# POOL issues a gather only when the third one in front of it has landed (graph kernel: two LSTM layers and a relational convolution)

## The chip, the cores and the metric

The kernel runs on one core of a Trainium2 chip. The metric is device time in microseconds, the median of the runs of one build: 597.44 us for the kernel before (three runs, 597.39 to 602.68). The names of the engines are those of the profile: PE (TensorE; PEld is its weight load), DVE (VectorE), ACT (ScalarE), POOL (GpSimd), SP (SyncE, which here only starts DMAs). Each has its own queue of instructions, and they meet through semaphores.

## The reference

Two graph layers, each with its own residual and layer norm. The first aggregates the neighbours with an LSTM, twice (weights `conv1`, `conv2`), the second multiplies each edge's source row with one of three relation matrices and sums over the target node.

```python
def _lstm_last(seq, wih, whh, bih, bhh):       # seq: 33 steps x 512 nodes x 128
    def step(carry, x_t):
        h, c = carry
        g = x_t @ wih.T + h @ whh.T + b
        i, f, gg, o = jnp.split(g, 4, axis=-1)
        c = sigmoid(f) * c + sigmoid(i) * jnp.tanh(gg)
        h = sigmoid(o) * jnp.tanh(c)
def _sage_conv(x, src, ...):
    msgs = x[src].reshape(n, d, c)             # 16896 edges = 512 nodes x 33
    aggr = _lstm_last(jnp.swapaxes(msgs, 0, 1), wih, whh, bih, bhh)
    return aggr @ wl.T + bl + x @ wr.T
# layer 1: _sage_conv, relu, _sage_conv; x = layernorm(x + that)
# layer 2: einsum('ni,rio->rno', x, weight); msg = hr[rel, src] * norm
#          h = segment_sum(msg, dst); out = layernorm(x + relu(h))
```

## The kernel before

**LSTM.** The input product of a step needs only the row of a node, so for each of the two LSTM layers `l` the table `gate_table[l]` (512 rows of 512 float32: all nodes times `wih`, plus the biases) is computed once, copied to `table_sb` in SBUF and stored to DRAM by SP. Step `t` then needs, for its 512 nodes, the table rows of their `t`-th neighbours. POOL fetches them with indirect DMAs ("gathers", line 442), four for each step (`K` = 4), 128 rows of 2 KB each, 256 KB in all, into `rows`. `rows` has `DEEP` = 5 turns of four slots, 20 slots (`SLOTS`), and each slot has its semaphore `rows_in[slot]`, which a gather raises by 16 when it has landed. Five of the 33 steps (0, 1, 3, 8 and 17, `BY_ONEHOT`) take their rows on PE with a one-hot matrix instead, so 28 steps of each layer are gathered: 56 turns, 224 gathers.

A turn's first gather waits, from the sixth turn on, for `gates1[1]` of the step that used the same slots five turns ago (line 440): PE raises it with the last recurrent product of a step (line 1066). The first gather of a layer waits for `table_stored`, and in layer 2 for both. The other three of a turn wait for nothing. So a layer begins with a run of 20 gathers, the whole depth of `rows`, and goes on with four for each finished step.

On PE a gathered step is 16 transposes of the gathered rows into the PSUM tile `gates` (line 1059), which wait for `rows_in`, for `if_ready` and `o_ready` (ACT has read what stood there), and then 24 products with `h_hi` and `h_lo` for each half of the step; the 512 nodes are two halves `h` of 256. With the fourth group of them it raises `gates0[h]` and `gates1[h]`. ACT makes of these the gates (`act_if`, `act_g`, `act_o`, lines 509 to 525) and tanh of the cell, DVE the cell and the new `h`, and PE waits for `h_hi_ready` and `h_lo_ready`. The two halves take turns: while ACT and DVE work on one, PE works on the other.

**Relational part.** 132 tiles of 128 edges, in 12 blocks. For 54 of the tiles PE picks the source rows with one-hots (line 1219, into PSUM, taken by ACT into `picked`, line 630) and multiplies them with the three matrices (line 1235). For the other 78 POOL gathers message rows from `msg_table` (line 453, 128 rows of 512 bytes, 64 KB) into `edge_rows`, two blocks deep, with a semaphore `edge_rows_in[c % 2][n]` for each place. From block 3 on a gather waits for `rows_taken` (ACT has read the place two blocks ago). PE sums all messages over the target nodes (line 1242).

POOL has nothing else to do than these 302 gathers, after a few small instructions at the start.

## Time and profile before

| | us |
|---|---|
| median of 3 runs (597.39 to 602.68) | 597.44 |
| the profiled execution's own time | 601.25 |
| its span, from first to last instruction | 599.2 |
| PE busy | 491.3 |
| DVE busy | 380.2 |
| ACT busy | 349.6 |
| POOL busy | 299.1 |
| software DMA queue (the gathers), share of 16 engines | 38.0% |

The profiled execution has 2.05 us outside its span (601.25 less 599.2) and is 3.81 us above the median. Its busy times say how long an engine had an instruction under way; a busy PE is not PE at its peak. Where an engine idled, the profile names what ended the idle time: another engine's instruction, a DMA, "issue" (nothing that the profile shows) or "remote" (an update that it can put down to no instruction near it).

### The profile page before, as it was taken

To read this page: it belongs to the slowest core of one execution; us is meant where nothing else is said; L and a number is where in the kernel's file an instruction comes from. 1 tells how busy PE (TensorE), PEld (TensorE's weight loads), DVE (VectorE), ACT (ScalarE), POOL (GpSimd) and SP (SyncE) were. 2 spreads that over 40 slices of the span, in tenths; PEclk is the share of its full clock that TensorE was granted. 3 is DMA by queue.
4 is the path that set the end of the run, shared out by engine and by line. 5 is a ranking of instruction groups with operands and counts; after the bars stand their busy time and mean duration, and the time that the engine had idled before them with its cause. 6 is when DMAs were issued, how large, how long until landed. Compare 5 with 4: busy or idle time off the path is not lost.

```text
span 599.2 us, 9532 instructions
## 1 busy us (share of the span) xinstructions
PE 491.3 (82%) x3479; PEld 349.7 (58%) x3479; DVE 380.2 (63%) x1040; ACT 349.6 (58%) x896; POOL 299.1 (50%) x312
## 2 busy tenths in 40 slices
PE   8638989788878799729898888878999649788696
PEld 3516767677767685518676667666775315444353
DVE  5306778668666685417677676766787329567384
ACT  4417767557666686417676576656776326447372
POOL 1662555564666500754646645666007746566620
PEclk9957999899999999958999999999999869899989
DMA  4862464574667601664646655666111211111100
GB/s 130 256 200 71 112 185 134 170 196 122 193 181 203 171 8 71 175 175 111 175 126 176 180 152 139 171 180 171 44 37 52 52 33 49 36 49 35 44 14 19
DMA packets 27833, 71.84 MB, mean 120 GB/s; under 512 B 6383, under 2 KB 10405, under 8 KB 27788
## 3 DMA queue, kind: packets, MB, share of 16 engines
q0 software_dynamic: 20416, 63.85, 38.0%
q1 hardware_dynamic: 6284, 6.48, 3.7%
q10 hardware_dynamic: 1088, 0.92, 0.5%
q8 instruction: 28, 0.46, 0.3%
q14 instruction: 17, 0.14, 0.1%
HBM read 68.06 MB, written 3.16 MB: 119 GB/s over the span
## 4 chain that ended last, share of the span: by engine, by line
PE 48%; ACT 17%; another core or an unknown queue 14%; DVE 13%; issue 7%; DVEq 0%; ACTq 0%
PE gates L1066 22%; PE gates L1059 6%; PE work L1242 5%; PE gates L1001 3%; ACT h_hi L505 3%; DVE h_full L756 3%; ACT act_g L521 3%; ACT act_if L509 2%; DVE h_lo L761 2%; DVE prod_ig L779 2%; DVE prod_fc L777 2%; ACT act_o L525 2%; PE gates L1219 2%; PE gates L1235 2%
## 5 line engine op out<-in xcount | busy, mean ns | idle before, releaser
L442 POOL DMA_INDIRECT rows<-gate_table,src_steps x224 | 216.9, 968 | 201.2 <-PE gates L1066 90.8
L1059 PE MATMUL gates<-ident,rows 128*128 128x128 f32 x896 | 122.9, 280 | 54.6 <-ACT act_o L525 29.3
L1059 PEld LDWEIGHTS gates<-ident,rows 128*128 128x128 f32 x896 | 100.2, 143 | 71.7 <-ACT act_o L525 37.2
L1066 PE MATMUL gates<-h_hi,whh_hi 128*128 128x256 f16 x512 | 127.9, 276 | 0.9
L1066 PE MATMUL gates<-h_hi,whh_lo 128*128 128x256 f16 x512 | 127.1, 275 | 0.0
L453 POOL DMA_INDIRECT edge_rows<-msg_table,msg_index x78 | 80.7, 1034 | 74.9 <-DMA msg_table<-table_sb 30.9
L1066 PE MATMUL gates<-h_lo,whh_hi 128*128 128x256 f16 x512 | 99.3, 276 | 0.9 <-DVE h_lo L761 0.9
L777 DVE TENSOR_TENSOR prod_fc<-act_if,cell 128x256 f32<-128x256 f32 x128 | 54.2, 424 | 68.0 <-issue 26.6
L509 ACT ACTIVATE act_if<-gates 128x512 f32<-128x512 f32 x112 | 66.0, 590 | 47.4 <-remote 35.6
L505 ACT ACTIVATE h_hi<-h_full 128x256 f16<-128x256 f32 x128 | 53.4, 417 | 47.2 <-DVE h_full L756 44.0
L779 DVE TENSOR_TENSOR prod_ig<-act_if,act_g 128x256 f32<-128x256 f32 x128 | 53.9, 421 | 37.9 <-issue 22.8
L761 DVE TENSOR_TENSOR h_lo<-h_full,h_hi 128x256 f16<-128x256 f32 x128 | 54.4, 425 | 31.8 <-ACT h_hi L505 18.1
L521 ACT ACTIVATE act_g<-gates 128x256 f32<-128x256 f32 x112 | 42.6, 380 | 33.1 <-PE gates L1066 24.0
L1066 PEld LDWEIGHTS gates<-h_hi,whh_hi 128*128 128x128 f16 x512 | 50.4, 98 | 19.0 <-ACT h_hi L505 10.0
L756 DVE SCALAR_TENSOR_TENSOR h_full<-act_o,tanh_c 128x256 f32<-128x256 f32 x132 | 55.3, 419 | 2.9 <-ACT tanh_c L501 2.4
L501 ACT ACTIVATE tanh_c<-cell 128x256 f32<-128x256 f32 x132 | 54.7, 414 | 1.7 <-DVE cell L785 1.2
L785 DVE TENSOR_TENSOR cell<-prod_ig,prod_fc 128x256 f32<-128x256 f32 x128 | 54.0, 422 | 2.2
L1066 PEld LDWEIGHTS gates<-h_hi,whh_lo 128*128 128x128 f16 x512 | 50.7, 99 | 5.7
L1066 PEld LDWEIGHTS gates<-h_lo,whh_hi 128*128 128x128 f16 x512 | 45.2, 98 | 14.0 <-DVE h_lo L761 1.2
L956 DVE TENSOR_TENSOR msg_lo<-msg_full,msg_hi 128x768 f16<-128x768 f32 (+2 forms) x23 | 21.3, 926 | 34.6 <-ACT msg_hi L657 33.8
L525 ACT ACTIVATE act_o<-gates 128x256 f32<-128x256 f32 x112 | 42.7, 381 | 0.0
L1242 PE MATMUL work<-rows,msg_lo 128*128 128x512 f16 x132 | 34.7, 390 | 8.2 <-issue 8.1
(158 smaller groups left out, 615.7 us busy)
## 6 DMA issues: line engine op xcount, KB each, us to landing
rows<-gate_table,src_steps POOLq DMA_INDIRECT x224
gate_table<-rows SPq DMA_DIRECT2D x8, 256.0 KB, 2.1
edge_rows<-msg_table,msg_index POOLq DMA_INDIRECT x78
code<-code_table SPq DMA_DIRECT2D x5, 160.0 KB
msg_table<-table_sb SPq DMA_DIRECT2D x4, 192.0 KB, 2.5
code<-code_table SPq DMA_DIRECT2D x5, 128.0 KB
whhT<-turned_whh SPq DMA_DIRECT2D x2, 256.0 KB, 2.6
wihT<-turned_wih ACTq DMA_DIRECT2D x1, 256.0 KB, 3.0
```

The lines of the kernel that those rows point to most:

```text
L442: pool.indirect_dma_start(rows[:, j * K + k, :], None, gate_table[l], bass.IndirectOffsetOnAxis(src_steps[:, t, k:k + 1], axis=0)).then_in ...
L453: pool.indirect_dma_start(edge_rows[:, c % 2, n, :], None, msg_rows, bass.IndirectOffsetOnAxis(msg_index[:, pool_first(c) + n:pool_first(c ...
L505: act.activation(h_hi[:, h, :], h_full[:, h, :], ACT.Copy).then_inc(h_hi_ready[h], 1)
L509: act.activation(act_if[:, h, :], gates[:, h, 0, :], ACT.Sigmoid, scale=1 / G_SCALE).then_inc(if_ready[h], 1)
L521: act.activation(act_g[:, h, :], gates[:, h, 1, 0:HN], ACT.Tanh, scale=1 / G_SCALE, bias=bias).then_inc(g_ready[h], 1)
L756: dve.scalar_tensor_tensor(h_full[:, h, :], act_o[:, h, :], H_SCALE, tanh_c[:, h, :], op0=ALU.mult, op1=ALU.mult).then_inc(h_full_ready[h], 1)
L761: dve.tensor_tensor(h_lo[:, h, :], h_full[:, h, :], h_hi[:, h, :], ALU.subtract).then_inc(h_lo_ready[h], 1)
L777: dve.tensor_tensor(prod_fc[:, h, :], act_if[:, h, HN:], cell[:, h, :], ALU.mult)
L779: dve.tensor_tensor(prod_ig[:, h, :], act_if[:, h, 0:HN], act_g[:, h, :], ALU.mult).then_inc(ig_ready[h], 1)
L1059: pe.matmul(gates[:, h, b, q * HN + k * P:q * HN + (k + 1) * P], rows[:, j * K + 2 * h + k, gate * P:(gate + 1) * P], ident[:, :], is_tran ...
L1066: mm = pe.matmul(gates[:, h, b, q * HN:(q + 1) * HN], w[:, gate * P:(gate + 1) * P], state[:, h, :], start=False, stop=last and q == 1, sk ...
L1242: mm = pe.matmul(work[:, 1, :], part[:, k % AHEAD, m, :], dst_onehot[k % AHEAD * GR + m], start=False, stop=False, skip_group_check=True)
```

## The change

A constant `IN_FLIGHT = 3` is added, and POOL waits before each gather, except the first three of each of the two loops, until the gather three places in front of it has landed. In the LSTM loop that order runs on over the turns and over both layers. The waits for slots that are to become free stay. No engine other than POOL gets, loses or moves an instruction.

```diff
+    IN_FLIGHT = 3
@@ gpsimd, LSTM gathers
                 for k in range(K):
+                    if turn * K + k >= IN_FLIGHT:
+                        landed, part = divmod(turn * K + k - IN_FLIGHT, K)
+                        pool.wait_ge(rows_in[landed % DEEP * K + part], 16 * (landed // DEEP + 1))
                     pool.indirect_dma_start(
                         rows[:, j * K + k, :], None, gate_table[l],
@@ gpsimd, gathers of the relational part
+            gathered = [(c, n) for c in range(BLOCKS) for n in range(SIZES[c] - PE_TILES[c])]
             for c in range(BLOCKS):
                 for n in range(SIZES[c] - PE_TILES[c]):
+                    if pool_first(c) + n >= IN_FLIGHT:
+                        landed, slot = gathered[pool_first(c) + n - IN_FLIGHT]
+                        pool.wait_ge(edge_rows_in[landed % 2][slot], 16 * slot_fills(landed, slot))
                     if c >= 3:
                         pool.wait_ge(rows_taken, pool_first(c - 2) + min(n + 1, SIZES[c - 2] - PE_TILES[c - 2]))
```

POOL's queue at the start of LSTM layer 1, before: the run of 20 gathers, and then one turn of four whose first waits for the step.

```order
L442 DMA rows<-gate_table,src_steps 128x512 [waits table_stored,src_loaded]
L442 DMA rows<-gate_table,src_steps 128x512 x19
L442 DMA rows<-gate_table,src_steps 128x512 [waits gates1_1]
L442 DMA rows<-gate_table,src_steps 128x512 x3
L442 DMA rows<-gate_table,src_steps 128x512 [waits gates1_1]
```

The same queue after the change, its first rows and those around the first gather that also waits for `gates1_1` (`rows_in0` to `rows_in19` are the landing semaphores of the 20 slots).

```order
L446 DMA rows<-gate_table,src_steps 128x512 [waits table_stored,src_loaded]
L446 DMA rows<-gate_table,src_steps 128x512 x2
L446 DMA rows<-gate_table,src_steps 128x512 [waits rows_in0]
L446 DMA rows<-gate_table,src_steps 128x512 [waits rows_in1]
```

```order
L446 DMA rows<-gate_table,src_steps 128x512 [waits rows_in16]
L446 DMA rows<-gate_table,src_steps 128x512 [waits rows_in17,gates1_1]
L446 DMA rows<-gate_table,src_steps 128x512 [waits rows_in18]
L446 DMA rows<-gate_table,src_steps 128x512 [waits rows_in19]
L446 DMA rows<-gate_table,src_steps 128x512 [waits rows_in0]
L446 DMA rows<-gate_table,src_steps 128x512 [waits rows_in1,gates1_1]
```

No gather moved. Of the run of 20 the first three are as before and the other 17 wait for a landing; each later gather waits for one too, and those that waited for a step now wait for both. In the relational part POOL's queue was this before (one row stands for 63 gathers):

```order
L453 DMA edge_rows<-msg_table,msg_index 128x128 [waits msg_stored,edge_ready]
L453 DMA edge_rows<-msg_table,msg_index 128x128 x14
L453 DMA edge_rows<-msg_table,msg_index 128x128 [waits rows_taken] x63
```

and is this after, at the place where the wait for `rows_taken` begins:

```order
L461 DMA edge_rows<-msg_table,msg_index 128x128 [waits edge_rows_in0_3]
L461 DMA edge_rows<-msg_table,msg_index 128x128 [waits edge_rows_in0_4]
L461 DMA edge_rows<-msg_table,msg_index 128x128 [waits rows_taken,edge_rows_in0_5]
L461 DMA edge_rows<-msg_table,msg_index 128x128 [waits rows_taken,edge_rows_in0_6]
L461 DMA edge_rows<-msg_table,msg_index 128x128 [waits rows_taken,edge_rows_in0_7]
```

The order of the gathers is the same there too; each of the last 75 of 78 has one wait more.

## Rows read from the trace of the kernel before

**Rows 1.** The page: its head, and busy us of each engine
```profile
span 599.2 us, 9532 instructions
PE 491.3 (82%) x3479; PEld 349.7 (58%) x3479; DVE 380.2 (63%) x1040; ACT 349.6 (58%) x896; POOL 299.1 (50%) x312
```

**Rows 2.** Waits of the whole span: engine line <- releaser: us in total, times, longest
```profile
POOL rows L442 <- PE gates L1066: 90.8, 41, 10.4
...
ACT act_if L509 <- remote: 35.6, 15, 7.2
...
ACT picked L630 <- remote: 29.0, 6, 11.1
...
POOL edge_rows L453 <- issue: 19.0, 61, 0.6
```

**Rows 3.** Stretches: one step with gathers, one without: busy us (instructions), PEclk, DMA, GB/s
```profile
171.39:177.36 5.97, 4.86 (x40) 3.90 (x40) 4.00 (x11) 3.75 (x11) 3.81 (x4) 1.00 0.62 177
212.99:217.53 4.54, 4.54 (x42) 3.95 (x41) 3.80 (x11) 3.74 (x11) 0.00 (x0) 1.00 0.08 22
```

**Rows 4.** Timeline (start, us) of the step with gathers, then of that without
```profile
175.27 0.38 PE L1066 MATMUL gates<-h_lo,whh_hi 128*128 128x256 f16 x2
...
177.13 0.38 ACT L521 ACTIVATE act_g<-gates 128x256 f32<-128x256 f32 x1 [0.87 <-PE gates L1066]
177.36 0.94 POOL L442 DMA_INDIRECT rows<-gate_table,src_steps  x1 [1.24 <-PE gates L1066]
...
215.69 0.38 PE L1066 MATMUL gates<-h_lo,whh_hi 128*128 128x256 f16 x2
...
216.11 0.38 ACT L521 ACTIVATE act_g<-gates 128x256 f32<-128x256 f32 x1
```

**Rows 5.** Timeline of POOL, first run of LSTM layer 1 and the turns behind it
```profile
17.24 1.12 POOL L442 DMA_INDIRECT rows<-gate_table,src_steps  x1 [14.89 <-DMA gate_table<-rows]
18.66 0.94 POOL L442 DMA_INDIRECT rows<-gate_table,src_steps  x1 [0.30 <-issue]
...
41.30 0.95 POOL L442 DMA_INDIRECT rows<-gate_table,src_steps  x1 [0.30 <-issue]
52.65 0.98 POOL L442 DMA_INDIRECT rows<-gate_table,src_steps  x1 [10.40 <-PE gates L1066]
...
56.44 0.95 POOL L442 DMA_INDIRECT rows<-gate_table,src_steps  x1 [0.30 <-issue]
```

**Rows 6.** Timeline of PE and ACT beside that run
```profile
24.67 0.38 PE L1066 MATMUL gates<-h_lo,whh_hi 128*128 128x256 f16 x2
27.16 0.60 ACT L485 ACTIVATE src_direct<-work 128x512 f16<-128x512 f32 x1 [5.44 <-remote]
...
43.38 0.84 ACT L515 ACTIVATE act_if<-gates,bias_cols 128x256 f32<-128x256 f32 x2 [8.29 <-issue]
```

**Rows 7.** Timeline of ACT and POOL, first run of LSTM layer 2
```profile
256.12 0.60 ACT L509 ACTIVATE act_if<-gates 128x512 f32<-128x512 f32 x1 [7.22 <-remote]
...
264.14 0.95 POOL L442 DMA_INDIRECT rows<-gate_table,src_steps  x1 [0.30 <-issue]
...
268.04 0.60 ACT L509 ACTIVATE act_if<-gates 128x512 f32<-128x512 f32 x1 [5.66 <-remote]
```

**Rows 8.** Timeline of the relational part: PE, ACT, and POOL's last gather
```profile
477.78 0.60 PE L1219 MATMUL gates<-pick_onehot,x_lo 128*128 128x256 f16 x4
...
491.09 1.30 ACT L630 ACTIVATE picked<-gates 128x768 f16<-128x768 f32 x2 [11.09 <-remote]
...
575.01 0.95 POOL L453 DMA_INDIRECT edge_rows<-msg_table,msg_index  x1 [0.30 <-ACT msg_full L648]
```

**Rows 9.** Stretches of 0.5 us, columns as in rows 3, behind a last gather
```profile
59.65:60.15 0.50, 0.38 (x4) 0.14 (x2) 0.50 (x3) 0.50 (x2) 0.00 (x0) 1.00 0.00 0
44.80:45.30 0.50, 0.50 (x4) 0.24 (x2) 0.00 (x0) 0.00 (x0) 0.00 (x0) 0.50 0.00 0
577.50:578.00 0.50, 0.50 (x6) 0.30 (x4) 0.42 (x3) 0.38 (x2) 0.00 (x0) 1.00 0.00 0
```

## The prediction

> **What bounds the kernel now.** I read the page first: PE is the busiest engine, 491.3 of 599.2 us, and POOL, the only engine that the change touches, is busy for half of it [rows 1]. Then two steps of the LSTM, one while POOL gathers and one after its last gather of a layer. The work is the same (40 and 42 matmuls), but the first takes 5.97 us and the second 4.54 [rows 3]. So a step loses 1.43 us to something that comes with the gathers, and it isn't that PE lacks its rows: they were fetched five turns earlier. The timeline says what is late [rows 4]. The last product of the step without gathers starts at 215.69 and lasts 0.38, and ACT starts on its result at 216.11, 0.04 us after its end. In the step with gathers the same product starts at 175.27 and would end at 175.65, but both engines that wait for its signal, ACT and POOL, start at 177.13 and 177.36: PE's signal is some 1.4 us late. That is the whole loss of the step.
>
> Where POOL issues without a pause the same lateness is far worse. In layer 1 the 20 gathers of the first run start at 17.24, 18.66 and so on to 41.30, 1.25 us apart with 0.30 idle between them [rows 5]. PE's last product for step 1 starts at 24.67, but ACT gets nothing from PE for 5.44 us up to 27.16, and later for 8.29 us up to 43.38 [rows 6]; POOL's wait for the next step's end, 10.40 us, ends at 52.65 [rows 5]. In layer 2 it is 7.22 and 5.66 us, the second ending at 268.04, just behind the last gather of that run at 264.14 [rows 7]. In the relational part a product of 477.78 reaches ACT at 491.09 [rows 8]. In total ACT waits 35.6 us at line 509 and 29.0 at line 630 for updates that the profile can put down to no instruction [rows 2]. The kernel is thus a chain PE, ACT, DVE, PE whose PE link is slow while gathers run. Whether the change helps depends on whether it alters that, and this depends first on whether its waits bind at all.
>
> **The change part by part.** It adds 221 waits in the LSTM loop (224 gathers less 3) and 75 in the relational one (78 less 3), all on POOL, and nothing else. Behind a waiting gather stand only gathers; PE waits for these in the LSTM, ACT in the relational part.
>
> *Does a wait bind?* POOL starts a gather 1.25 us behind the last one, so the one three in front started 3.75 us ago (3 x 1.25). From a signal to POOL's start take 0.25 us, worked out from ACT and POOL: they wait for the same one, and POOL starts 0.23 us behind ACT, 177.36 to 177.13 [rows 4]. A wait therefore binds when a gather lands later than 3.50 us after its start (3.75 less 0.25). No row gives a landing, so I bound it by the moment at which the DMA engines fall silent behind a last gather. The last of a turn of four starts at 56.44 and nothing moves from 59.65 on: at most 3.21 us for its data [rows 5, 9]. The last of the run of 20 starts at 41.30, and nothing moves from 44.80 on: at most 3.50 us [rows 5, 9]. The last of the relational part, a quarter of the bytes, starts at 575.01 and is silent by 577.50: at most 2.49 [rows 8, 9]. The signal may come a little behind the data. So in the LSTM the landing is 3.2 to 3.5 us and perhaps some tenths, right at the threshold, and in the relational part a full microsecond below it.
>
> *Relational part:* no wait binds, 0 us. A wait that is met costs nothing that shows: 61 of its gathers, most of which already carry the wait for `rows_taken`, start after 19.0 us of idle in all, 0.31 each [rows 2], against the 0.30 of gathers without a wait [rows 5].
>
> *A turn of four in steady state:* the next turn starts 5.97 us behind the last one [rows 3], so its first three gathers wait for landings of 4.72 to 5.97 us and less ago, all past. Only the fourth (3.75 us behind the first of its own turn) is near. If it is late by some tenths, four turns of slots lie filled in front of it; 0 us. Its cover is this lead: were it gone, each turn would cost what the wait costs.
>
> *The two runs of 20:* 17 gathers of each wait for a landing. If each lands at 3.50 or sooner the cost is 0. If each takes 3.75 us until its signal, three gathers take 4.00 instead of 3.75, 0.083 us for each gather, 1.4 us for 17, 2.8 for both runs. The landing bounds lie nearer to the first case, but the signal behind the data speaks for the second, so I take half, 0.7 for each run. Is it on the path? ACT came free of its long waits when the run was over or nearly so [rows 6, 7], so I count it: 1.4 us in all.
>
> *PE's late signals:* the rows say that they don't come from many gathers in flight. In steady state, at 175.27, three at most are under way, and the signal is 1.4 us late all the same [rows 4]; in the relational part each is gone after 2.49 us, so two are in flight, and there the delay is 13 us [rows 8, 9]. A limit of three doesn't reach this. I count 0 us, with the gain of the rival below as its other bound.
>
> The Trainium skill (DMA: Bandwidth & Descriptors, Anatomy of one DMA — SWDGE (gpsimd) path) gives a fixed 2.0 us and bytes at 436 GB/s for such a DMA. By it, an estimate for 256 KB, a gather lands after 2.6 us, no wait would bind anywhere and the sum would be 0; the silent stretches allow up to 3.50 us here, so I don't go by it.
>
> *Sum:* 0 + 0 + 1.4 + 0. The profiled execution takes 601.25 (span 599.2 and 2.05 around it) and would take 602.65; it stands 3.81 above the median of the runs, so the median goes from 597.44 to 598.8.
>
> **The rivals.**
>
> *Faster: the pauses let PE through.* Against it stands the argument on two or three in flight; for it, that PE's lateness grows with the length of POOL's unbroken run (1.4 us in a turn of four, 5 to 8 in the runs of 20), so something may fill up in them, and a few tenths of pause for each gather could keep it from filling. The prize: in layer 1 ACT's 5.44 + 8.29, in layer 2 its 7.22 + 5.66, 26.6 us in all, if only the runs are cured [rows 6, 7]. All of it gives 572; half, which is more likely of a pause this short, 585.5. If the steps of 5.97 us came down too, each would give up to 1.43 us, some 46 of them another 66 us, down to 506; nothing makes the pauses bind there, so I leave that out of the range.
>
> *Slower: the landing signal is later than the silence of the DMA engines shows.* If POOL sees a landing 4.5 us after the start, three gathers take 4.75 instead of 3.75. Then a run of 20 takes 5.7 us more (17 x 0.33), 11.3 for both, and the fourth gather of each turn is 1.0 us late; the relational waits still don't bind (2.49 + 1.0 is under 3.50). With the lead of the slots lasting, this gives 597.44 + 11.3 = 608.8. It decides from a landing of some 4.0 us on, where the two runs cost 6 us together (34 x 0.17). If moreover PE's signal hangs on the end of a turn's last gather (that ended at 176.12, which is 177.36 less the idle 1.24, and ACT had the signal 1.0 us later [rows 4]), 46 turns add 46 us; nothing but that one coincidence speaks for it.
>
> The Trainium skill (same page, Rules for kernel authors) says to issue a DMA early and wait on its semaphore late, so that the fixed cost is hidden; a wait at the next issue but two does the opposite, which is this rival's case.
>
> *No effect at all:* every landing is below 3.50 and the waits are met; 597.4. The forecast holds it.
>
> **How the numbers follow.** About 1% (6 us) is what a measurement of this kernel can tell from no change; one of its three runs was 602.68. The forecast with no effect in it, 594 to 603: 0.58. Pauses help PE by more than 6 us: 0.25, since the lateness is large and its cause isn't known. Slower by more than 6 us: 0.17. The time is that of the likeliest, 598.8. The range goes down to 580, which leaves out the full cure of the runs and more (0.1), and up to 609, the second rival's own time (0.07 beyond). The likeliest case's own range is 595 to 603.
>
> **What would show it.** POOL's waits of the runs should name the landing of `rows` and stay at some tenths each; the last gather of the first run should start 0 to 2 us later against its first than the 24.06 us of now (41.30 less 17.24). The relational gathers should keep their 0.30 us. ACT's waits of 5 to 8 us beside the runs, and the step of 5.97 us, should be there as before. If the step is shorter or those waits are gone, the argument on the number in flight was wrong; if POOL's gathers are a microsecond or more further apart, the landing bound was.

## The result, and the profile after

| | this kernel | the kernel before, beside it | ratio, 95% interval |
|---|---|---|---|
| median of 20 runs each, us | 600.23 (587.98 to 609.30) | 600.80 (595.81 to 607.54) | 0.9878 [0.9842, 0.9915] |
| the profiled execution, us | 596.03 (span 594.1) | 601.25 (span 599.2) | |

By the ratio the changed kernel is 1.2% faster. The ratio compares fast runs alone, those near each kernel's fastest, and of the changed kernel these are only 7 of the 20 (587.98 to 596.27). Over all 20 runs the medians differ by 0.1% and the means (598.73 and 600.75) by 2.0 us, with a 95% interval from 5.1 us faster to 1.0 us slower. A second measurement of the same kernel (e5 below) gave a ratio of 0.9937 [0.9895, 0.9979], from 6 of its 10 runs, and means over all runs that differ by 0.4 us (605.38 and 605.81). So there is a gain of at most some 1%, and all runs taken together don't show one. What differs plainly is the scatter: a standard deviation of 5.8 us in place of 3.2.

The page and the waits of the kernel after (engine, line <- releaser: us in total, times, longest):

```profile
span 594.1 us, 9645 instructions
PE 499.3 (84%) x3479; PEld 355.4 (60%) x3479; DVE 382.5 (64%) x1040; ACT 352.6 (59%) x896; POOL 303.9 (51%) x312
```
```profile
POOL rows L446 <- PE gates L1074: 58.3, 23, 7.4
POOL rows L446 <- issue: 56.9, 168, 1.4
ACT act_if L517 <- remote: 34.9, 16, 4.2
...
ACT picked L638 <- remote: 27.1, 6, 12.5
...
POOL rows L446 <- DMA rows<-gate_table,src_steps: 23.0, 22, 2.3
```

Beside [rows 1, 2]: only 22 of the 221 waits in the LSTM show as waits for a landing, 23.0 us together. POOL's wait for PE fell from 90.8 to 58.3 us. ACT's unexplained waits at lines 517 and 638 are about as large in total as before, but the longest at 517 is 4.2 us in place of 7.2 (at 638 it is 12.5 in place of 11.1). The relational part hardly moved: 147.9 us from its first gather to the end before (599.2 less 451.3), 149.0 after (594.1 less 445.1).

POOL in LSTM layer 1, after (start, us, instruction, [idle before, releaser]): the first and fourth gather, one in the middle, the last of the run of 20, the first of the sixth and of the seventh turn, and the first of the layer's last turn:

```profile
16.88 1.12 POOL L446 DMA_INDIRECT rows<-gate_table,src_steps  x1 [14.53 <-DMA gate_table<-rows]
...
22.80 0.95 POOL L446 DMA_INDIRECT rows<-gate_table,src_steps  x1 [2.29 <-DMA rows<-gate_table,src_steps]
...
33.29 0.95 POOL L446 DMA_INDIRECT rows<-gate_table,src_steps  x1 [0.47 <-DMA rows<-gate_table,src_steps]
...
43.85 0.95 POOL L446 DMA_INDIRECT rows<-gate_table,src_steps  x1 [0.49 <-DMA rows<-gate_table,src_steps]
47.14 0.94 POOL L446 DMA_INDIRECT rows<-gate_table,src_steps  x1 [2.35 <-remote]
...
59.06 0.99 POOL L446 DMA_INDIRECT rows<-gate_table,src_steps  x1 [7.21 <-PE gates L1074]
...
199.71 0.95 POOL L446 DMA_INDIRECT rows<-gate_table,src_steps  x1 [0.83 <-DMA rows<-gate_table,src_steps]
```

Before, the sixth turn began at 52.65 [rows 5]; the seventh and the last of the layer began here:

```profile
64.01 0.99 POOL L442 DMA_INDIRECT rows<-gate_table,src_steps  x1 [6.62 <-PE gates L1066]
...
201.29 0.94 POOL L442 DMA_INDIRECT rows<-gate_table,src_steps  x1 [1.26 <-PE gates L1066]
```

The run of 20 is now 26.97 us long from first to last start (43.85 less 16.88) in place of 24.06, and yet the kernel is 5.15 us ahead at the sixth turn relative to its first gather (30.26 against 35.41 us), and 4.6 at the seventh. PE's lateness is smaller beside the run: in the same 38 us PE does 172 instructions, where it did 141 before (the row of before stands with e7 below; the columns are those of rows 3).

```profile
17.00:55.00 38.00, 25.03 (x172) 18.29 (x171) 15.57 (x40) 17.77 (x46) 22.91 (x24) 0.78 0.66 188
```

Before, ACT's long waits there were 5.44 and 8.29 [rows 6] and between them a third:

```profile
34.25 0.47 ACT L521 ACTIVATE act_g<-gates,bias_cols 128x256 f32<-128x256 f32 x1 [4.79 <-remote]
```

After, there are four shorter ones, 15.2 us in all in place of 18.5:

```profile
32.81 0.60 ACT L493 ACTIVATE src_direct<-work 128x512 f16<-128x512 f32 x1 [4.40 <-remote]
38.49 0.38 ACT L529 ACTIVATE act_g<-gates 128x256 f32<-128x256 f32 x1 [3.63 <-remote]
43.39 0.60 ACT L517 ACTIVATE act_if<-gates 128x512 f32<-128x512 f32 x1 [4.25 <-remote]
46.91 0.39 ACT L529 ACTIVATE act_g<-gates 128x256 f32<-128x256 f32 x1 [2.92 <-remote]
```

By the layer's last turn 1.2 us of the lead are left (182.83 us from the first gather against 184.05). Between the seventh turn and the last one the steady turns gave 3.4 us back: by POOL's timeline most turns there now take 5.6 to 7.2 us, and in some a gather waits for a landing (0.83 at 199.71), where before most took 5.9 to 6.0. Behind the last turn the kernel wins again. From first gather to first gather layer 1 takes 218.85 us in place of 222.42, layer 2 209.3 in place of 211.7, and the first gather of all comes 0.36 us sooner; with the 1.1 us that the relational part lost this makes the 5.1 us between the two spans.

### The profile page after: what moved, and what is told of

Same layout as the page of the kernel before. It is cut to its first block, busy times and chain, and to the rows that moved or that the text cites. A ratio compares the mean times of both kernels' runs of the same rounds, so it can differ in the third digit from the quotient of the medians.

```text
span 594.1 us, 9645 instructions
## 1 busy us (share of the span) xinstructions
PE 499.3 (84%) x3479; PEld 355.4 (60%) x3479; DVE 382.5 (64%) x1040; ACT 352.6 (59%) x896; POOL 303.9 (51%) x312
## 4 chain that ended last, share of the span: by engine, by line
PE 54%; ACT 16%; another core or an unknown queue 13%; DVE 11%; issue 6%; DVEq 0%; ACTq 0%
PE gates L1074 24%; PE gates L1067 8%; PE work L1250 6%; PE gates L1009 3%; ACT act_g L529 2%; ACT h_hi L513 2%; ACT act_if L517 2%; DVE msg_full L947 2%; PE gates L1227 2%; PE work L1001 2%; DVE h_full L764 2%; PE gates L1243 2%; ACT act_o L533 2%; DVE prod_ig L787 2%
## 5 line engine op out<-in xcount | busy, mean ns | idle before, releaser
L446 POOL DMA_INDIRECT rows<-gate_table,src_steps x224 | 218.5, 976 | 195.0 <-PE gates L1074 58.3
L1067 PE MATMUL gates<-ident,rows 128*128 128x128 f32 x896 | 124.6, 282 | 41.4 <-ACT act_o L533 18.7
L1067 PEld LDWEIGHTS gates<-ident,rows 128*128 128x128 f32 x896 | 101.4, 144 | 59.1 <-issue 30.0
L1074 PE MATMUL gates<-h_hi,whh_hi 128*128 128x256 f16 x512 | 132.4, 284 | 0.9
L1074 PE MATMUL gates<-h_hi,whh_lo 128*128 128x256 f16 x512 | 131.3, 282 | 0.0
L461 POOL DMA_INDIRECT edge_rows<-msg_table,msg_index x78 | 83.8, 1074 | 68.3 <-DMA msg_table<-table_sb 29.1
L1074 PE MATMUL gates<-h_lo,whh_hi 128*128 128x256 f16 x512 | 101.7, 282 | 0.3 <-issue 0.3
L1074 PEld LDWEIGHTS gates<-h_hi,whh_hi 128*128 128x128 f16 x512 | 51.9, 101 | 18.7 <-ACT h_hi L513 9.4
L1074 PEld LDWEIGHTS gates<-h_hi,whh_lo 128*128 128x128 f16 x512 | 52.1, 102 | 7.1
L1074 PEld LDWEIGHTS gates<-h_lo,whh_hi 128*128 128x128 f16 x512 | 46.8, 100 | 14.0 <-issue 0.6
```

The lines of the kernel that those rows point to most:

```text
L446: pool.indirect_dma_start(rows[:, j * K + k, :], None, gate_table[l], bass.IndirectOffsetOnAxis(src_steps[:, t, k:k + 1], axis=0)).then_in ...
L461: pool.indirect_dma_start(edge_rows[:, c % 2, n, :], None, msg_rows, bass.IndirectOffsetOnAxis(msg_index[:, pool_first(c) + n:pool_first(c ...
L1067: pe.matmul(gates[:, h, b, q * HN + k * P:q * HN + (k + 1) * P], rows[:, j * K + 2 * h + k, gate * P:(gate + 1) * P], ident[:, :], is_tran ...
L1074: mm = pe.matmul(gates[:, h, b, q * HN:(q + 1) * HN], w[:, gate * P:(gate + 1) * P], state[:, h, :], start=False, stop=last and q == 1, sk ...
```

## The experiments

Two kinds of chip turned up. On one the kernel before takes about 600 us, as in the result; on the other it takes 471 to 473 us. Which kind a set of runs met was chance, and it is the largest effect in this study. The quick kind was met on two chips (one of them twice: e1 to e4, then e9 to e12), the slow kind on three and in the result. A comparison below is always between kernels on the same chip. The times are medians of all runs. Three runs stand far out and are in no ratio: 1665.52 us of e1, 1665.68 of e11, and 685.53 of the kernel before beside s4 to s6.

| run | what it is | this, us | before, same chip | ratio, 95% interval |
|---|---|---|---|---|
| e1 | waits in the LSTM alone | 514.21 | 472.83 | 1.0825 [1.0769, 1.0881] |
| e12 | the same again | 507.84 | 471.30 | 1.0757 [1.0688, 1.0826] |
| e2 | waits in the relational part alone | 475.95 | 472.83 | 1.0047 [1.0012, 1.0082] |
| e3 | two in flight, everywhere | 649.15 | 472.83 | 1.3753 [1.3695, 1.3811] |
| e4 | three in flight in each layer's first five turns | 473.42 | 472.83 | 1.0014 [0.9989, 1.0040] |
| e9 | two in flight in each layer's first five turns | 486.83 | 471.30 | 1.0306 [1.0241, 1.0370] |
| e10 | third gather of a turn waits for PE | 468.89 | 471.30 | 0.9928 [0.9897, 0.9958] |
| e11 | e9 and e10 together | 487.34 | 471.30 | 1.0334 [1.0285, 1.0383] |
| s4 | memset of 128x8 behind each LSTM gather | 496.52 (its other run: 521.60) | 470.97 | no ratio |
| s5 | memset of 128x128 | 512.18 | 470.97 | 1.0913 [1.0739, 1.1088] |
| s6 | memset of 128x384 | 557.22 | 470.97 | 1.1873 [1.1689, 1.2057] |
| e5 | the change as it is, again | 604.91 | 605.61 | 0.9937 [0.9895, 0.9979] |
| e6 | gathers of a quarter of the bytes | 597.55 | 599.59 | one run each |
| e7 | LSTM rows by plain DMAs of SP | 502.34 | 599.59 | one run each |
| e8 | two in flight, everywhere | 642.16 | 599.59 | one run each |
| s1 | as e10 | 602.30 | 608.67 | 0.9895 [0.9836, 0.9954] |
| s2 | as e9 | 604.87 | 608.67 | 0.9945 [0.9899, 0.9990] |
| s3 | as e11 | 603.32 | 608.67 | 0.9892 [0.9848, 0.9936] |

### e1 to e4: on a chip where PE's signals are not late

e1 removes the relational wait, e2 the LSTM wait; e3 and e4 are these edits of the changed kernel:

```diff
-    IN_FLIGHT = 3
+    IN_FLIGHT = 2
```
```diff
-                    if turn * K + k >= IN_FLIGHT:
+                    if turn * K + k >= IN_FLIGHT and turn % (T - 1 - len(DIRECT)) < DEEP:
```

(e4 has no relational waits.)

> Theory A (a landing that comes late holds POOL for a moment, and PE's late signals in the LSTM get shorter by it; the relational waits never bind, since a 64 KB gather is in by 2.5 us of the 3.5 that it has): this kernel, which has the waits of the LSTM loop alone, equals the whole change, ratio 0.985 to 0.998 to the kernel before. Rival B (the waits bind too seldom to do anything, the difference is the scatter of the runs): 0.997 to 1.003.

> Only the 75 waits of the relational part. Theory A: they never bind, ratio 0.998 to 1.002, POOL's idle time at these gathers 0.30 us each as before. Rival C (the relational part is where the gain comes from): 0.985 to 0.995.

> IN_FLIGHT = 2 in both loops. A gather then starts at best 3.0 + 0.25 us behind the second in front, 1.63 us each instead of 1.25. Theory A: PE's late signals come from gathers that follow each other without a pause, so with a pause of 0.4 us behind each the waits of 5 to 8 us beside the runs of 20 shrink to under 3 us, and the step of 5.97 us gets shorter; 0.97 to 0.99 overall, if POOL's own 6.5 us for four gathers does not become the bound of a step (then 1.02 to 1.05). Rival B (the lateness has nothing to do with the spacing): the LSTM steps go from 5.97 to 6.5 us, 46 turns by 0.55 us or 25 us more, ratio 1.04.

> Waits for a landing only in the first five turns of each LSTM layer (the runs of 20 gathers), none in the later turns and none in the relational part. Theory A with the gain in the runs: the same ratio as with all waits, 0.985 to 0.995, PE's waits beside the runs shorter than before by 3 us or more in each layer, the rest unchanged. If the gain comes from the later turns: 0.998 to 1.003.

All four met the chip of 473 us, for which none of the expectations was made. There the LSTM waits cost 8%, all of it outside the runs of 20 (e4: 1.0014). The waits of e1, and of e3 (us in total, times, longest):

```profile
POOL rows L446 <- DMA rows<-gate_table,src_steps: 61.6, 62, 3.0
...
PE gates L1064 <- issue: 32.4, 35, 1.9
```
```profile
POOL rows L446 <- DMA rows<-gate_table,src_steps: 202.0, 175, 3.4
```

More than half of POOL's waits for a landing in e1 come up as PE's waits before the transposes of the rows (line 1064; 0.3 us in all in e4). The reason that there is no room for them can be seen in e4, in whose steady turns nothing waits for a landing. Its page, and its POOL from the sixth turn on:

```profile
PE 455.8 (97%) x3479; PEld 345.1 (74%) x3479; DVE 379.3 (81%) x1040; ACT 351.4 (75%) x896; POOL 302.4 (65%) x312
```
```profile
43.25 0.94 POOL L446 DMA_INDIRECT rows<-gate_table,src_steps  x1 [0.30 <-issue]
44.49 0.95 POOL L446 DMA_INDIRECT rows<-gate_table,src_steps  x1 [0.30 <-issue]
```

PE is busy 97% of the span, with the same 3479 matmuls, and POOL goes from gather to gather with 0.30 us between: a turn is 4 x 1.25 = 5.0 us of POOL against the 4.54 us that a step takes without gathers [rows 3], and only the five steps that need no gather keep POOL up with PE. Gathers are all but the bound here, and a pause of theirs costs. e2's interval lies above 1 too: on this chip the relational waits cost 2.2 us (0.0047 x 472.83), though in its trace no relational gather of POOL waits for a landing.

### s4 to s6: the spacing alone

To set the spacing without a wait for landings, a memset follows every LSTM gather, and POOL waits for its end:

```diff
+                    pool.memset(spare[:, :], 0.0).then_inc(spare_set, 1)
+                    pool.wait_ge(spare_set, turn * K + k + 1)
```

> The kernel before with a memset of 128x8 behind each of the 224 LSTM gathers, whose end POOL waits for: about 1.6 us from gather to gather in place of 1.25. On a chip of about 600 us: if the spacing is what delays PE's signals, the pause of 10 us behind the run of 20 shrinks and the steps become POOL's own 4 x 1.6 = 6.4 us or PE's 4.5 to 5, whichever is longer; 112 gathers x 1.6 = 179 us and the four steps without gathers hidden beside them, some 185 us per layer in place of 222 and 212: 540 us. If the count of gathers per step is what costs, the step of 5.97 us only grows: 600 to 615. On a chip of about 471 us (layers of some 160 us): POOL becomes the bound, 490 to 520.

> The same with a memset of 128x128: about 1.7 us from gather to gather. On a chip of about 600 us by spacing: 112 x 1.7 = 190 us and 196 per layer, 560 us; by count 605 to 620. On a chip of about 471 us: 500 to 530.

> The same with a memset of 128x384: about 2.0 us from gather to gather, as two in flight gave. On either chip POOL's stream is the bound: 112 x 2.0 = 224 us per layer, 600 to 620 on a chip of about 600 us; 560 to 590 on a chip of about 471 us.

These too met a chip of the quick kind. The added pause came out smaller than expected; POOL in s4:

```profile
100.17 0.95 POOL L444 DMA_INDIRECT rows<-gate_table,src_steps  x1 [0.27 <-POOL spare L448]
...
101.51 0.95 POOL L444 DMA_INDIRECT rows<-gate_table,src_steps  x1 [0.27 <-POOL spare L448]
```

Inside a string of gathers the spacing is mostly 1.34 us in s4 and, from the same view, 1.44 in s5 and 1.65 in s6, where 1.6 was expected of s4 and 2.0 of s6. From s5 to s6 that is 224 x 0.21 = 47 us more of POOL, and the span grew by 43.9 (554.7 less 510.8). On this kind of chip nearly every us added to POOL's stream is a us of the kernel, so POOL's stream costs time there without any wait for a landing. Whether this spacing would help on a chip of 600 us was their question, and that stays unanswered.

### e5 to e8: on chips of 600 us

e5 is the changed kernel. e6 leaves three quarters of each row ungathered and feeds PE the same quarter for all four gates; e7 replaces the LSTM gathers with plain DMAs of the same bytes, issued by SP, of rows that are not the neighbours' (POOL issues the few loads of `code` that SP had). Neither computes the reference's result.

```diff
-                        rows[:, j * K + k, :], None, gate_table[l],
+                        rows[:, j * K + k, 0:P], None, gate_table[l].rearrange("n (q c) -> (n q) c", c=P),
```
```diff
-                    pool.indirect_dma_start(
-                        rows[:, j * K + k, :], None, gate_table[l],
-                        bass.IndirectOffsetOnAxis(src_steps[:, t, k:k + 1], axis=0)
-                        ).then_inc(rows_in[j * K + k], 16)
+                    sp.dma_start(rows[:, j * K + k, :], gate_table[l][k * P:(k + 1) * P, :]).then_inc(rows_in[j * K + k], 16)
```

e8 is e3's edit.

> The whole change again, beside the kernel before on the same chip. The chip of the first four experiments ran the kernel before in 472.83 us, not 597 to 601, and there PE's signals were not late. If this run meets such a chip (before near 473 us): theory D (where PE keeps up, POOL's stream of gathers is what bounds the LSTM, landings take 3.9 us and a wait for the third in front binds in most gathers) gives 1.08 to 1.09, the ratio of the kernel with the LSTM waits alone. If it meets one where before takes about 600 us: theory A and rival B give 0.985 to 1.003.

> The kernel before, but each LSTM gather moves 128 rows of 512 bytes instead of 2048 (64 KB, the same number of rows and of gathers, source rows 0 to 511 of the table seen as 2048 rows of 128), and PE transposes these 128 columns for all four gates; the output is not the reference's. Where PE's signals are late (kernel before near 600 us): theory E (the lateness comes from the bytes that land in SBUF) expects steps of about 4.6 us instead of 5.97 and some 500 us or less; rival F (it comes from issuing the gathers and handling their rows, whatever their size, as in the relational part) expects steps of 5.9 us and 590 to 600 us. Where they are not late (before near 473 us): the landing falls from 3.9 to under 3 us and the time stays within 5 us of 473.

> The LSTM rows are loaded by SP with plain DMAs (table rows k x 128 and on, not the neighbours' rows; the output is not the reference's), the same bytes in the same number of 2 KB rows, with the waits of the kernel before; POOL issues the code loads that SP had. Where PE's signals are late (before near 600 us): rival F in the form that POOL's making of the descriptors delays PE expects steps near 4.6 us and ACT's waits of 5 to 8 us beside the first 20 loads gone, 500 us or less; theory E (bytes into SBUF) expects the steps of 5.9 us to stay. Where they are not late (before near 473 us): PE stays busy, 450 to 475 us.

> IN_FLIGHT = 2 in both loops, a second time, for the kind of chip where PE's signals are late. On the other kind it took 649 us against 473. There (before near 600 us) theory A (the spacing lets PE through) expects ACT's waits of 5 to 8 us beside the runs of 20 under 3 us each, and 580 to 640 us in all since POOL now needs 6.5 to 8 us for a turn; rival B (spacing changes nothing about PE) expects these waits as long as before, and 650 us or more.

**The local lead, a second time.** e5 has the same edits as the change, and its POOL begins layer 1 and its sixth turn here:

```profile
17.02 1.12 POOL L446 DMA_INDIRECT rows<-gate_table,src_steps  x1 [14.67 <-DMA gate_table<-rows]
...
45.74 0.94 POOL L446 DMA_INDIRECT rows<-gate_table,src_steps  x1 [0.60 <-issue]
```

The sixth turn comes 28.72 us behind the first gather. In the three traces whose first run has no landing waits it is 35.41 (before), 35.71 (e6) and 35.64 (s1); in the result it was 30.26. So this lead is larger than what sets those three apart (0.3 us). But it doesn't last: e5's layer 1 takes 222.49 us, against 222.42, 221.60 and 222.70 in those three, and its layer 2 218.96 against 211.68, 212.89 and 214.50. This execution took 610.91 us and was one of e5's slower ones. What the lead is worth at the end of a layer is thus 3.6 us in one trace and nothing in the other. By the expectation, e5 was to lie between 0.985 and 1.003 under both of its theories, so it doesn't choose between them.

**Not the bytes, and not the number in flight.** In e6, POOL's last gather of the run, and the first of each of the next three turns:

```profile
38.59 0.95 POOL L442 DMA_INDIRECT rows<-gate_table,src_steps  x1 [0.30 <-issue]
50.32 0.98 POOL L442 DMA_INDIRECT rows<-gate_table,src_steps  x1 [10.78 <-PE gates L1066]
...
61.64 0.99 POOL L442 DMA_INDIRECT rows<-gate_table,src_steps  x1 [6.58 <-PE gates L1066]
...
67.58 0.95 POOL L442 DMA_INDIRECT rows<-gate_table,src_steps  x1 [1.20 <-PE gates L1066]
```

With 27.8 MB moved in place of 71.8, the wait behind the run (10.78 against 10.40 us [rows 5]), the 5.94 us turn and the 1.20 us of idle in front of it are all as before. Its small gathers are also soon over. Behind the last of the run, nothing moves from here on:

```profile
41.00:41.50 0.50, 0.00 (x0) 0.00 (x0) 0.00 (x0) 0.07 (x1) 0.00 (x0) 0.50 0.00 0
```

That is at most 2.41 us after its start at 38.59, so with 1.25 us from gather to gather no more than two are in flight, as in e8 below, and the lateness is there in full. Two in flight is not what ends it in e8.

**It comes with POOL's gathers.** The granted clock isn't the cause: it was 1.00 in the step of 5.97 us [rows 3]. Stretches of the kernel before, then of e7, whose LSTM has none (busy us and instructions of PE, PEld, DVE, ACT, POOL; then PEclk, DMA share, GB/s):

```profile
17.00:55.00 38.00, 23.03 (x141) 15.84 (x140) 12.40 (x31) 13.78 (x34) 21.15 (x22) 0.69 0.56 168
...
95.00:235.00 140.00, 121.02 (x956) 95.36 (x955) 96.79 (x254) 91.93 (x243) 68.33 (x71) 0.99 0.53 151
```
```profile
17.00:55.00 38.00, 37.68 (x316) 31.08 (x315) 29.70 (x80) 30.50 (x80) 0.73 (x1) 1.00 0.79 266
...
95.00:235.00 140.00, 139.48 (x1158) 115.27 (x1156) 112.01 (x292) 111.15 (x289) 4.29 (x8) 1.00 0.55 182
```

PE does 316 instructions instead of 141 beside the first run, and 1158 instead of 956 in the long stretch, while the DMA engines move more (266 against 168 GB/s). e7 changes several things at once, the engine that issues, the kind of DMA and the order of the rows, and doesn't say which of them it is. Nor was DVE tried as a part of it. The relational part of e7 still gathers on POOL, and there ACT's unexplained wait is as in [rows 2]:

```profile
ACT picked L627 <- remote: 32.8, 7, 13.9
```

**Pauses end it, and then cost more.** e8: POOL's first run, stretches, and waits:

```profile
34.33 0.97 POOL L446 DMA_INDIRECT rows<-gate_table,src_steps  x1 [0.87 <-DMA rows<-gate_table,src_steps]
36.08 0.94 POOL L446 DMA_INDIRECT rows<-gate_table,src_steps  x1 [0.78 <-DMA rows<-gate_table,src_steps]
```
```profile
17.00:55.00 38.00, 34.59 (x282) 28.60 (x281) 26.68 (x71) 27.72 (x73) 19.70 (x20) 0.96 0.54 150
...
95.00:235.00 140.00, 99.73 (x744) 83.01 (x743) 75.52 (x195) 73.71 (x186) 68.01 (x69) 0.88 0.50 138
```
```profile
POOL rows L446 <- DMA rows<-gate_table,src_steps: 195.7, 157, 3.6
```

Beside the first run PE does 282 instructions in 38 us, twice what it did before, with 1.95 us from gather to gather in the mean (37.13 us from first to last start). In the steady turns it does 744 in place of 956: four gathers now mostly take 7.5 to 8.2 us. The 642.16 us lie just above the 640 that the spacing theory allowed, and below the 650 of its rival. It fits with this that two in flight takes 642 us here and 649 on the other kind of chip: with PE's signals on time and POOL's stream as the bound, the two kinds would hardly differ. In the relational part POOL has more room, and there two in flight gained. Before, then e8, from the first relational gather to the end:

```profile
451.30:599.20 147.90, 115.30 (x606) 59.83 (x604) 89.35 (x271) 72.09 (x177) 80.66 (x78) 0.92 0.15 37
```
```profile
505.80:640.20 134.40, 113.00 (x613) 59.47 (x610) 89.75 (x274) 73.94 (x179) 84.37 (x78) 0.95 0.16 41
```
```profile
ACT picked L638 <- remote: 2.9, 1, 2.9
```

It takes 13.5 us less than in the kernel before (11.9 less than e6's 146.3 us on the same chip, whose relational part is unchanged), and ACT's unexplained wait at that line falls from 29.0 us [rows 2] to 2.9. Its gathers are 1.45 us apart in the median in place of 1.25. Two in flight in the relational part alone was not tried by itself.

### e9 to e12 and s1 to s3: the runs of 20 and the turns of four apart

e9 and s2 keep two in flight in the first five turns of a layer and have no other wait. e10 and s1 are the kernel before with one wait per turn; e11 and s3 have both:

```diff
                 for k in range(K):
+                    if k == 2 and turn >= DEEP and fetched[turn - DEEP + 1][0] == l:
+                        pool.wait_ge(gates1[0], steps_done(*fetched[turn - DEEP + 1]))
```

> The whole waits are taken out again, and instead POOL keeps two gathers in flight in the first five turns of each layer alone; the later turns and the relational part go as before the change. On a chip where the kernel before takes about 600 us: if what delays PE's signals in a run of 20 is that its gathers follow each other 1.25 us apart, ACT's waits of 5 to 8 us beside the two runs go (some 13 + 13 us of waits, of which a part is PE's own work that comes up), the run itself takes about 20 x 1.9 = 38 us and not 25, which the five turns that it serves cover; 590 to 596 us, ratio 0.982 to 0.993. If the lateness is no matter of spacing, or the run's later end holds PE up (rows of turns 2 to 4 come late), 598 to 605. On a chip where the kernel before takes about 473 us there is no lateness to remove: 472 to 477.

> The kernel before, with one wait per turn from the sixth of a layer on: the third gather of a turn is issued when PE has finished half 0 of the next step, so that a turn's four gathers come as two and two, about half a step (3 us) apart; nothing waits for a landing. On a chip of about 600 us: if a bunch of four delays PE's signals and two do not, the step of 5.97 us falls towards the 4.5 us of a step without gathers; with 29 such steps per layer up to 29 x 2 x 0.7 = 40 us, so 560 to 590 us. If it is the number of gathers per step and not their bunching, the step stays 5.9 us and the time 597 to 602. On a chip of about 473 us nothing is late and POOL has less slack for gathers of 3.9 us that go unpaced: 472 to 478.

> Both edits of the two kernels ahead of it. If both delays are one mechanism (gathers close to each other), the gains add up: the sum of the two differences from the kernel before, within 2 us. If only the runs or only the turns matter, the time is that of the one that gained. On a chip of about 473 us: 472 to 479.

> The change's waits in the LSTM loop alone, as in the second kind of chip's first run of it. On a chip of about 600 us: if the whole change's gain comes from the LSTM (222.4 to 218.9 us in layer 1 and 211.7 to 209.3 us in layer 2 in its profiled run, against 147.9 to 149.0 us in the relational part), this is at the whole's ratio or up to 0.002 below it, 0.985 to 0.994. If the gain came from the relational part it is 1.00. On a chip of about 473 us it is 1.08 again, since gathers that take 3.9 us each at three in flight bound the step.

> The kernel that parts a turn's four gathers into two and two, half a step apart, with no wait on a landing. If this is a chip of about 600 us: a bunch of four that delays PE's signals, and two that do not, give 560 to 590 us; the number of gathers per step as the cause gives 597 to 602. If it is a chip of about 471 us: 0.993 again.

> Two gathers in flight in the first five turns of each layer, nothing else. If this is a chip of about 600 us: the late signals beside the runs of 20 go, 590 to 596 us; if the pauses hold PE up at the run's end by as much as they save, as they do by 15 us on the other kind of chip (486.8 against 471.3 us), 600 to 612. On a chip of about 471 us: 1.03 again.

> Both. On a chip of about 600 us: the sum of the two differences if they are one mechanism that acts at two places. On a chip of about 471 us: 1.03 again.

e12 repeated e1. e10 is 0.7% faster on the quick chip, where 472 to 478 us were expected; its POOL hardly waits for PE at all, and why it gains wasn't pursued. e9 and e11 missed too: up to 477 and 479 us were expected there, and they took 15.5 and 16.0 us more than the kernel before, all of it in the two LSTM layers by their traces, beside e10's. On the chip of 609 us s1, s2 and s3 gained 1.05%, 0.55% and 1.08%. s2 missed its 590 to 596 us, and the gains of s1 and s2 don't add up in s3. s1 fell far short of the 560 to 590 us that it was to reach if bunches were the cause, and yet it gained as much as the change did, with no wait in the run of 20 and none for a landing; why wasn't found. For the bunch wasn't parted. POOL in s1, the third gather of a turn and the ones behind it:

```profile
61.53 1.18 POOL L444 DMA_INDIRECT rows<-gate_table,src_steps  x1 [6.82 <-PE gates L1068]
63.01 0.95 POOL L444 DMA_INDIRECT rows<-gate_table,src_steps  x1 [0.30 <-issue]
...
67.63 0.95 POOL L444 DMA_INDIRECT rows<-gate_table,src_steps  x1 [1.17 <-remote]
```

The wait of the third gather ends (61.53, 67.63), then it, the fourth and the next turn's first two go without a pause, four in a row as ever, and PE's next signal arrives 1.17 us behind the last. The gate had moved by two gathers and nothing else; s1 therefore says nothing on spacing. It does show what PE's signal goes by. In the kernel before, POOL's idle time in front of a turn is 1.05 to 1.35 us in 35 of the 44 turns behind the sixth, in e6 as well; here the string ends two gathers later in the turn, and the signal again comes 1.17 us behind its end.

s3 shows where the gain of slowing the run goes. Stretches of s3, then its POOL, the first gather of the unpaced turns, the last before a pause, and the next:

```profile
17.00:55.00 38.00, 34.05 (x288) 28.23 (x287) 27.36 (x74) 28.46 (x75) 19.71 (x20) 1.00 0.53 147
55.00:95.00 40.00, 25.77 (x173) 19.62 (x170) 16.55 (x44) 15.48 (x41) 21.60 (x24) 0.74 0.54 160
```
```profile
55.36 1.08 POOL L448 DMA_INDIRECT rows<-gate_table,src_steps  x1 [0.30 <-issue]
...
76.92 0.94 POOL L448 DMA_INDIRECT rows<-gate_table,src_steps  x1 [0.30 <-issue]
88.60 0.98 POOL L448 DMA_INDIRECT rows<-gate_table,src_steps  x1 [10.73 <-PE gates L1073]
```

In the paced run PE does 288 instructions instead of 141. But when the pacing ends at 55.36, several turns of slots are already free, POOL issues 18 gathers without a pause up to 76.92, and the wait of 10.7 us for PE that used to stand behind the run of 20 stands behind these 18. PE does 173 instructions in the next 40 us; the kernel before does this:

```profile
55.00:95.00 40.00, 35.80 (x298) 28.81 (x297) 29.98 (x82) 28.97 (x79) 18.61 (x20) 1.00 0.48 135
```

Of the 147 instructions won, 125 are lost again. So in these traces the delay goes with a long unbroken string of gathers, and not with the start of a layer.

## Why the prediction was off

**What bounds the kernel** was read rightly for this chip: PE's signals are late beside POOL's gathers, and without gathers the lateness is gone (e7, 97 us faster). That this could depend on the chip was in no view of one profile.

**Whether a wait binds.** The waits did bind, as the threshold of 3.50 us has it; the landing was taken too short. Of the run's first gather POOL saw the landing 5.67 us after its start (22.80 less 16.88 less the 0.25 for the signal), where three in flight cost a wait of 2.29 us at one stroke, and the prediction had no term for it. The gather of 33.29 waited for that of 29.37, its landing seen after 3.67 us (3.92 less 0.25), and that of 43.85 for 39.90, after 3.70. The silence of the DMA engines gave 3.21 to 3.50 [rows 9], so by this estimate the signal comes some 0.2 us behind. The run got 2.91 us longer where 1.4 were allowed as the upper case, 0.7 counted. The Trainium skill's figure (DMA: Bandwidth & Descriptors, Anatomy of one DMA), 2.6 us as an estimate, is contradicted here: by it none of these waits would have bound.

**The relational part** was counted at 0, and it came out a little above: 1.1 us longer in the profile, 150.4 us in e5's trace against 146.3 to 148.7 in the six traces of chips of 600 us without these waits (before, e6, e7, s1, s2, s3), and 2.2 us on the quick chip (e2). POOL hardly waits for a landing there, as was foreseen; where the rest comes from isn't known.

**The turns of four** were counted at 0, since "four turns of slots lie filled in front of it". The turns gave back 3.4 us of layer 1's lead. It is not the rows that come late but PE's next signal: behind an unbroken string of gathers POOL mostly idles 1.05 to 1.35 us for it. The second rival named that and called it a coincidence; s1 shows that it is none. A wait inside a turn isn't a full loss, though: in the changed kernel's traces, where a gather of a turn had waited a microsecond for a landing, the pause in front of the next turn was mostly down to 0.3 to 0.4 us, so the signal had come in the meantime. (A small slip beside it: the gathers of a turn wait for one that started 4.72 us ago, each of the first three, not 4.72 to 5.97.) On the quick chip the same term is 36 to 41 us (e1, e12), since there POOL has no slack (e4).

**PE's late signals** is the step that failed: "the rows say that they don't come from many gathers in flight … A limit of three doesn't reach this. I count 0 us". The premise stands (e6: two in flight, and late all the same), but the conclusion doesn't follow. The waits don't only limit the number in flight, they put pauses in the string, and e8 and s3 show that with an idle time of 0.9 to 1.0 us in front of each gather, in the mean, PE does twice the work beside a run of layer 1. In the changed kernel one wait of 2.29 us and up to 0.2 us more at seven others brought the sixth turn of layer 1 forward by 5.15 us in spite of a longer run, and by some 7 us in e5. Which of these pauses did it isn't shown. The first rival named precisely this ("something may fill up in them") and was right in kind and too high in size: 5.15 us at the first run where 13.7 were at stake (18.5 with the wait of 4.79 that the rows left out), and 5.1 us of the whole span where its lower price was 13.3. The turns of four that follow, whose strings the change hardly parts, kept their lateness.

**The number:** 598.8 us was forecast and 600.23 measured, with a kernel before that measured 600.80 beside it and 597.44 earlier. That the two numbers are close is in part luck, since the run's longer landings and PE's earlier signals, both missed, go against each other. What was wrong is the sign: a loss of 0.2% was forecast, and the ratio shows a gain of 1.2%. As said with the result, that gain rests on 7 of 20 runs. The step is shown wrong by where PE stands at the sixth turn in two traces, and only weakly by the total.

What stays open: how much of the ratio comes from the waits in the LSTM (e1 and e12, which were to tell, met the quick kind of chip); what it is, between POOL's indirect DMAs and PE's signals, that fills up; why some chips don't show it; and whether a spacing below the 1.95 us of e8, without a wait for landings, would be enough on a chip of 600 us. By an estimate, a spacing of 1.5 us would fill 6.0 us of a turn, which is what a turn takes there now.

## What to carry to other kernels

When an engine's signal is late beside another engine's string of DMA issues, ask how long the string runs without a pause, not only how many transfers are under way. In these runs a pause helped only where the issuing engine had slack; before pacing it, add up its issue time per turn (here 5.0 us) against the step it serves (4.5 to 6.0 us). And a cure at one place is to be followed to the next string: slots that came free in the meantime turn it into a new one (s3). Last, read a lead inside one trace as just that, until the times of all runs bear it out.

## What the runs showed of the hardware

The same kernel takes 471 to 473 us on some chips and 600 to 609 on others, at a mean granted clock of 0.992 to 0.999 on the former and 0.93 to 0.95 on the latter. The difference goes with PE's signals beside POOL's gathers. On the slower kind they come 1.4 us late in a turn of four gathers [rows 4], and in layer 1 POOL waits 10 to 11 us for one behind 18 or 20 in a row (before, e6, s1, s3), whatever the bytes; in layer 2 the wait behind the run is 3.3 us before and 3.9 in e6. A change worth 1% or nothing on the one kind costs about 8% on the other through its LSTM part alone, so a measured gain of this sort should not be taken over to another chip without a run there.
